# A sorted mixture of experts: inverting the order on chip, and one indirect DMA a block each way

## The reference

```python
x = x + tanh(g_xattn[0]) * attention(layernorm(x), ctx_768, ...)   # 16 heads, 1601 keys a batch
x = x + tanh(g_ffn[0]) * ffn(layernorm(x), ...)

def ffn(x, ...):                        # 8 experts, inner size 512
    shared = expert(x, Wg_s, Wu_s, Wd_s)   # silu(x @ Wg.T) * (x @ Wu.T) @ Wd.T
    probs = sigmoid(x @ Wr.T + rb)
    scores, idx = top_k(probs, 2)
    cw = (one_hot(idx, 8) * scores[..., None]).sum(-2)
    out = shared
    for e in range(8):
        out = out + cw[..., e:e + 1] * expert(x, Wg[e], Wu[e], Wd[e])
    return out
```

## Time and profile before

| | |
|---|---|
| time, median of 3 runs | 1178.47 us (1176.94 to 1181.26) |
| profiled execution, device time | 1180.16 us |
| its span | 1178.4 us |
| its mean granted TensorE clock | 0.957 |
| PE busy | 1095.5 us, 93% |
| DVE busy | 657.3 us, 56% |
| ACT busy | 570.7 us, 48% |
| POOL busy | 136.2 us, 12% |

### The profile page before, as it was taken

The page is one execution under the profiler, slowest core; times in us unless marked ns, Lnnn a source line. Parts: engine busy times, 40 slices in busy tenths (PEclk is TensorE's granted clock), DMA queues, the critical chain, the costliest instruction groups (busy, mean ns, idle before and its releaser), DMA issues. The chain is left out here.

```text
span 1178.4 us, 15206 instructions
## 1 busy us (share of the span) xinstructions
PE 1095.5 (93%) x5534; PEld 534.8 (45%) x5534; DVE 657.3 (56%) x895; ACT 570.7 (48%) x1056; POOL 136.2 (12%) x156
## 2 busy tenths in 40 slices
PE   4879999999999999999999999978869999999983
PEld 2433335434434433534433433435536666666652
DVE  4598776886676787677797685103412222222245
ACT  2107776776676776567777577623111111111110
POOL 4500000020000002000000003200550000000055
PEclk9859999999999999999999999859989999999998
DMA  9753505531505532505333501005820111111125
GB/s 314 114 93 38 60 1 61 102 46 16 61 1 60 96 39 30 61 1 60 38 41 45 59 3 59 5 5 174 321 94 18 45 45 45 46 45 45 36 72 151
DMA packets 51129, 78.08 MB, mean 66 GB/s; under 512 B 10993, under 2 KB 36210, under 8 KB 51058
## 3 DMA queue, kind: packets, MB, share of 16 engines
q1 hardware_dynamic: 45184, 66.87, 29.9%
q0 software_dynamic: 3072, 8.39, 2.2%
q10 hardware_dynamic: 2802, 1.85, 0.6%
HBM read 32.34 MB, written 16.52 MB: 41 GB/s over the span
## 5 line engine op out<-in xcount | busy, mean ns | idle before, releaser
L521 ACT ACTIVATE probs<-ring_ps 128x512 f32<-128x512 f32 (+1 forms) x832 | 443.4, 597 | 184.4 <-PE ring_ps L651 179.9
L755 DVE TENSOR_REDUCE mpart<-s_ps 128x2 f32<-128x1024 f32 x384 | 457.9, 1219 | 100.4 <-PE s_ps L638 98.9
L651 PE MATMUL ring_ps<-qst,kst 64*128 64x512 f32 (+1 forms) x832 | 233.8, 471 | 3.7 <-ACT probs L521 3.1
L666 PE MATMUL pv_ps<-probs,vp 128*32 128x512 f32 (+2 forms) x1664 | 226.2, 617 | 0.7 <-ACT probs L521 0.7
L638 PE MATMUL s_ps<-kst,qst 63*128 63x512 f32 (+1 forms) x1024 | 194.2, 419 | 11.8 <-DVE mpart L755 11.6
L651 PEld LDWEIGHTS ring_ps<-qst,kst 64*128 64x128 f32 (+1 forms) x832 | 102.4, 183 | 216.5 <-ACT probs L521 98.8
L962 ACT ACTIVATE s_sb<-gu_ps 128x512 f32<-128x512 f32 x55 | 32.8, 597 | 277.6 <-PE gu_ps L1039 277.6
L1039 PE MATMUL gu_ps<-wgu,xbT 128*128 x312 | 140.3, 593 | 0.0
L638 PEld LDWEIGHTS s_ps<-kst,qst 63*128 63x128 f32 x1024 | 95.6, 194 | 90.6 <-DVE mpart L755 68.9
L1168 DVE TENSOR_TENSOR h_sb<-s_sb,gu_ps 128x512 f32<-128x512 f32 x55 | 37.8, 687 | 174.8 <-ACT s_sb L962 174.8
L430 POOL COPY rspread<-rden 128x512 f32<-128x512 f32 x16 | 9.8, 612 | 674.6 <-DVE rden L798 674.6
(11 more groups left out here) (128 smaller groups left out, 712.2 us busy)
## 6 DMA issues: line engine op xcount, KB each, us to landing
kst<-parts SPq DMA_DIRECT2D x64, 200.5 KB, 4.4
kst<-parts SPq DMA_DIRECT2D x64, 100.2 KB, 4.2
sorted_x<-zeros SPq DMA_DIRECT2D x1, 4992.0 KB, 19.7
xb<-sorted_x SPq DMA_DIRECT2D x39, 128.0 KB, 2.2
sorted_y<-ysb SPq DMA_DIRECT2D x39, 128.0 KB, 1.7
qst<-parts SPq DMA_DIRECT2D x64, 64.0 KB, 4.2
wgu<-in_WgT SPq DMA_DIRECT2D x16, 256.0 KB, 7.9
wgu<-in_WuT SPq DMA_DIRECT2D x16, 256.0 KB, 8.1
```

Of the source, the lines that this page charges most:

```text
L521: nc.scalar.activation(probs[0:w, m % NPB, h, :], ring_ps[0:w, bank(("st", idx)), :], ACT.Exp, scale=SCALE).then_inc(exp_done, 1)
L651: nc.tensor.matmul(ring_ps[0:w, bank(("st", idx)), :], kst[u % NKB][rows, h // 2, mt * P:mt * P + w], qst[u % NKB][rows, h // 2, :], start ...
L666: last = nc.tensor.matmul(pv_ps[32 * h:32 * h + c1 - c0, :], values[:, c0:c1], probs[0:w, m % NPB, h, :], start=(mt == 0), stop=(mt == MT ...
L755: nc.vector.tensor_reduce(mpart[:, heads, t, q], s_ps[:, n % NSP], AX.X, ALU.max).then_inc(s_free, 1)
```

## The change

The scattered copy of the rows is gone. The normalised rows are stored to DRAM in token order (`rows`), 12 tiles by one DMA of SP during the last unit of attention and the last four by ACT in step 0. The sorted order is turned round on chip: for each of the 32 (choice, tile) pairs DVE makes two one-hot tiles from the slots, 128x128 (the row in a block) and 128x40 (the block, times the pair's number), and PE adds up the 32 products (`inverse`, before gate_up(4)), which gives for every row of every block the number of the pair it holds, or zero for padding. `make_lists` makes `token` (which row to fetch) and `target` (where its result goes) from it. Eight one-hot pairs are made in step 2 (ring of `NHOT` = 8), 24 in step 4.

GpSimd then fetches each block with one gather from `rows` by `token` and stores its result with one scatter to `picked` by `target`, where results lie in the order (choice, token); padding rows go to places of their own behind. SP does no block DMAs any more. When all scatters have landed it reads `picked` back in eight plain DMAs of 512 KB into the space of four experts' weights. Seven shared tiles stand before the blocks and nine after (`EARLY` = 7); combines are spread over seven steps from the fourth step after the last block's first; output stores come in the order in which tiles are finished. The clearing of the DRAM buffer is gone.

```diff
-NYG = 4
-EARLY = 10
-GATHER_ORDER = list(range(EARLY, TT)) + list(range(EARLY))
+EARLY = 7
+ASIDE = EARLY + 2
+COMBINE_ORDER = list(range(ASIDE, TT)) + list(range(ASIDE))
+SLOTS = TOP * B * N
+NCOL = NBLK + NBLK % 2
+NHOT = 8
 LAST = slice(TT - NT, TT)
-AT_LOGITS, AT_RANKS = 1, 2
+AT_LOGITS, AT_RANKS, AT_INVERSE = 1, 2, 4
 STK = 3 * HD
 NKB = 3
     return i - NBLK if i >= EARLY + NBLK else None
+
+
+def combines(i):
+
+    step, steps = i - (EARLY + NBLK + 3), TT - EARLY - 2
+    return range(TT * step // steps, TT * (step + 1) // steps) if 0 <= step < steps else range(0)
+
+
+def stores():
+
+    done = []
+    for i in range(TT + NBLK + 2):
+        done += [(COMBINE_ORDER[n], "combined", n + 1) for n in combines(i) if COMBINE_ORDER[n] < ASIDE]
+        t = tile_of(i - 2) if i >= 2 else None
+        if t is not None and t >= ASIDE:
+            done.append((t, "y_out", i - 1))
+    return done
 
...
                                  mneg[NT * h:NT * (h + 1), :].bitcast(F32)).then_inc(row_loaded[u % NKB], 16)
 
             sp.wait_ge(pool_ready, 3)
-                         zeros[:, None, :].to_broadcast([P, NBLK, D])).then_inc(zeroed, 16)
...
                     load_rows(u + 1)
+                else:
+                    sp.wait_ge(xn2_ready, NT * (B - 1))
+                    sp.dma_start(rows_dram[0:LAST.start * P, :].rearrange("(t p) d -> p t d", p=P),
+                                 xn2[:, 0:LAST.start, :]).then_inc(rows_stored, 16)
                 if hg == 2 and b + 2 < B:
                     load_ctx(b + 2)
...
+        hot_blk = sb("hot_blk", [P, NHOT, NCOL], F32R)
+        hot_row = sb("hot_row", [P, NHOT, P], F32R)
+        picked = wgu[:, 0:B].rearrange("p b k n -> p b (k n)").rearrange("p b (c t d) -> p b c t d", c=2, d=D)
...
 
-            def load_block(r):
-                if r >= NXB:
-                    sp.wait_ge(t_full, r - NXB + 1)
-                sp.dma_start(xb[:, r % NXB, :], xg_dram[r * P:(r + 1) * P, :]).then_inc(xb_loaded[r % NXB], 16)
-
-            sp.wait_ge(scattered, 16 * 2 * TT)
-            for r in range(NXB - 1):
-                load_block(r)
-            for r in range(NBLK):
-                if r + NXB - 1 < NBLK:
-                    load_block(r + NXB - 1)
-                sp.wait_ge(y_out, EARLY + r + 1)
-                sp.dma_start(yg_dram[r * P:(r + 1) * P, :], ysb[:, r % NXB, :]).then_inc(y_stored[r % NXB], 16)
-            for n, t in enumerate(GATHER_ORDER[TT - EARLY:]):
-                sp.wait_ge(combined, TT - EARLY + n + 1)
-                sp.dma_start(O["out"][t // NT, (t % NT) * P:(t % NT + 1) * P, :], x1[:, t, :]).then_inc(out_done, 16)
-            for n, t in enumerate(range(EARLY, TT)):
-                sp.wait_ge(y_out, EARLY + NBLK + n + 1)
+            for i in range(NXB):
+                sp.wait_ge(y_stored[i], 16 * ((NBLK - 1 - i) // NXB + 1))
+            for b in sorted(range(B), key=lambda b: COMBINE_ORDER.index(b * NT + NT - 1)):
+                for c in range(2):
+                    at = c * B * N + b * N
+                    sp.dma_start(picked[:, b, c], picked_dram[at:at + N, :].rearrange("(t p) d -> p t d", p=P)
+                                 ).then_inc(picked_loaded[b], 16)
+            for t, engine_sem, count in stores():
+                sp.wait_ge(combined if engine_sem == "combined" else y_out, count)
                 sp.dma_start(O["out"][t // NT, (t % NT) * P:(t % NT + 1) * P, :], x1[:, t, :]).then_inc(out_done, 16)
             sp.wait_ge(out_done, 16 * TT)
 
         @block.gpsimd
         def _(pool):
             nc.gpsimd.memset(ones[:], 1.0).then_inc(consts, 1)
-            nc.gpsimd.iota(count_i[:], pattern=[[1, NBLK]], base=0, channel_multiplier=0).then_inc(consts, 1)
+            nc.gpsimd.iota(count_i[:], pattern=[[1, NCOL]], base=0, channel_multiplier=0).then_inc(consts, 1)
 
             nc.gpsimd.iota(tri_i[:], pattern=[[1, E], [-1, E]], base=0, channel_multiplier=0).then_inc(consts, 1)
             pool.wait_ge(consts, 3)
 
             nc.gpsimd.affine_select(out=lower[:], in_=ones[:], compare_op=ALU.is_gt, fill=0.0, base=0,
                                     pattern=[[1, P]], channel_multiplier=-1).then_inc(consts, 1)
+            nc.gpsimd.iota(col_i[:], pattern=[[1, P]], base=0, channel_multiplier=0).then_inc(consts, 1)
+            nc.gpsimd.iota(id_i[:], pattern=[[B * N, 2], [P, TT]], base=1, channel_multiplier=1).then_inc(consts, 1)
+            nc.gpsimd.iota(trash_i[:], pattern=[[P, NBLK]], base=SLOTS + 1, channel_multiplier=1).then_inc(consts, 1)
             rstd_on_pool(nc, pool, LAST, mv, veps, rstd, power, ln, 1, sq, 0)
-            pool.wait_ge(xn2_ready, NT)
-            pool.wait_ge(slots_ready, 1)
-            for t in range(TT):
-                for c in range(2):
-                    pool.indirect_dma_start(xg_dram[:], bass.IndirectOffsetOnAxis(ap=slot_i[:, c, t:t + 1], axis=0),
-                                            xn2[:, t, :], None).then_inc(scattered, 16)
-            for i in range(NXB):
-                pool.wait_ge(y_stored[i], 16 * ((NBLK - 1 - i) // NXB + 1))
-            for n, t in enumerate(GATHER_ORDER):
-                if n >= NYG:
-                    pool.wait_ge(combined, n - NYG + 1)
-                for c in range(2):
-                    pool.indirect_dma_start(yg[:, n % NYG, c, :], None, yg_dram[:],
-                                            bass.IndirectOffsetOnAxis(ap=slot_i[:, c, t:t + 1], axis=0)
-                                            ).then_inc(gathered[n % NYG], 16)
+
+            def gather(r):
+                if r >= NXB:
+                    pool.wait_ge(t_full, r - NXB + 1)
+                pool.indirect_dma_start(xb[:, r % NXB, :], None, rows_dram[:],
+                                        bass.IndirectOffsetOnAxis(ap=token[:, r:r + 1], axis=0)
+                                        ).then_inc(xb_loaded[r % NXB], 16)
+
+            pool.wait_ge(rows_stored, 16)
+            pool.wait_ge(token_ready, 1)
+            for r in range(NXB - 1):
+                gather(r)
+            pool.wait_ge(target_ready, 1)
+            for r in range(NBLK):
+                if r + NXB - 1 < NBLK:
+                    gather(r + NXB - 1)
+                pool.wait_ge(y_out, EARLY + r + 1)
+                pool.indirect_dma_start(picked_dram[:], bass.IndirectOffsetOnAxis(ap=target[:, r:r + 1], axis=0),
+                                        ysb[:, r % NXB, :], None).then_inc(y_stored[r % NXB], 16)
 
         @block.scalar
         def _(act):
...
                     silu(i)
+                if i == 0:
+                    act.wait_ge(xn2_ready, NT)
+                    act.dma_start(rows_dram[LAST.start * P:LAST.stop * P, :].rearrange("(t p) d -> p t d", p=P),
+                                  xn2[:, LAST, :]).then_inc(rows_stored, 16)
                 if i >= 1:
                     take_ht(i - 1)
...
                 nc.tensor.matmul(t_ps[:, at + n:at + 2 * n], ones[:], flat, start=True, stop=True
                                  ).then_inc(rank_full, 1)
+
+            def inverse():
+                at = 3 * TT * E
+                for n in range(2 * TT):
+                    pe.wait_ge(hot_ready, n + 1)
...
 
             for i in range(JOBS + 2):
+                if i == AT_INVERSE:
+                    inverse()
...
-            dve.wait_ge(consts, 4)
+            dve.wait_ge(consts, 7)
+            nc.vector.tensor_copy(col[:], col_i[:])
...
                     own(nc.vector.tensor_reduce(slot_f[:, c], pick[:], AX.X, ALU.add))
-                nc.vector.tensor_copy(slot_i[:], slot_f[:]).then_inc(slots_ready, 1)
-
-                own(nc.vector.tensor_tensor(past[:, :, 0:E - 1], rows_f[:, :, None].to_broadcast([P, NBLK, E - 1]),
+                own(nc.vector.tensor_copy(slot_i[:], slot_f[:]))
+                own(nc.vector.tensor_scalar(lane_i[:], slot_i[:], P - 1, None, ALU.bitwise_and))
+                own(nc.vector.tensor_copy(lane[:], lane_i[:]))
+                own(nc.vector.tensor_tensor(first_row[:], slot_f[:], lane[:], ALU.subtract))
+
+            def make_hot(jobs):
+
+                for n in jobs:
+                    c, t = divmod(n, TT)
+                    if n >= NHOT:
+                        dve.wait_ge(hot_used, n - NHOT + 1)
+                    nc.vector.tensor_scalar(hot_row[:, n % NHOT, :], col[:], lane[:, c, t:t + 1], None, ALU.is_equal)
+                    nc.vector.tensor_scalar(hot_blk[:, n % NHOT, :], rows_f[:], first_row[:, c, t:t + 1],
+                                            ids[:, c, t:t + 1], ALU.is_equal, ALU.mult).then_inc(hot_ready, 1)
+
+            def make_lists():
+
+                dve.wait_ge(hot_used, 2 * TT)
+                own(nc.vector.tensor_copy(held[:], t_ps[:, 3 * TT * E:3 * TT * E + NBLK]))
+                own(nc.vector.tensor_scalar(second[:], held[:], float(B * N), float(-B * N), ALU.is_gt, ALU.mult))
```

(44 more changed lines are left out.)

35 lines of the change are left out of this document (23 added, 12 removed).

## The result

On the chip of the prediction's runs the changed kernel takes 1210.46 us (median of 4 runs, 1208.67 to 1215.59) and the kernel before 1177.70 (4 runs, 1173.60 to 1181.26): ratio 1.0286, 95% interval 1.024 to 1.0333. It is slower by 2.9%, as forecast (1218, range 1186 to 1236). On another chip, on which the kernel before takes longer, the ratio is 1.0164 (see the experiments). The profiled execution took 1211.1 us, with a span of 1209.4.

A forecast was written before the change was run, and what follows sets the result against it. PE bounds the kernel, so its standstills in the expert stage count: +63.4 blocks, -2.7 old stalls, -2.2 head, -16.6 tail, -2.4 stores = +39.5; 1180.16 becomes 1219.7, minus 1.7 gives 1218 us, range 1186 to 1236.

The forecast's parts named there:

- Blocks: Expert blocks: take_y to landed block exceeds the allowed 3.17 us by 1.81, period 7.63, 35 x 1.81 = +63.4; old stalls replaced, -2.7.
- 4.98 us "word for word": Blocks: release-to-data time of two indirect DMAs behind one wait, read from the old read back, taken as the new chain.
- half case: Blocks: GpSimd wakes quickly, chain 4.10 us, +32.6 instead of +63.4, time 1187; chance 0.17 (1184 to 1208).
- main case: Blocks: chain from take_y to data near 5 us, time 1208 to 1232; chance 0.62.
- the quick wake: Blocks: GpSimd starts at the release, chain 4.10 us, +32.6, time 1187; range 1184 to 1208, chance 0.17.
- Hidden wait: Blocks, rival: descriptor preparation or generation overlaps, chain within 3.17 us, period 5.82, sum -23.9, time 1155; chance 0.13.
- Clock: Blocks, rival: idle PE drops to 1.2 GHz in each block, +1.7 a block, 60 in all, 1278; chance 0.05.
- Head: List stage before the blocks: inverse costs +11.1, lost stall gives -13.3, together -2.2, between -4 and +2.
- The stall of 13.3: List stage: PE time lost around 32 indirect scatters before the first block, expected to go entirely.
- The upper bound of the prediction (+2): Head: worst end of -4 to +2, with pairs at 0.41 us and PE perhaps returning at lower clock, 1.4.
- Tail and stores: After the blocks: 16.6 of 21.2 us lost come back; one final store left instead of six, -2.4.
- Attention: Before the experts: dropping the 5 MB clear (19.7 us to land) and storing rows during attention each change 0.

## Why the prediction was right

**Blocks: the mechanism right, its price too high.** Forecast 35 waits and a period of 7.63; measured 35 and, typically, 7.03. The term that was mis-sized is the choice of 4.98 us "word for word" for the chain from take_y to data. Gather after scatter (1.29) and rows after the gather (2.78) came as read from the earlier trace rows; the start of the scatter came 0.28 after its release and not 0.88. The two places that gave 0.88 and 0.90 were waits of GpSimd for several semaphores, and two waits in place of one give the dearer start back in the changed kernel. So the chain is 4.36, 1.19 over what is free, and 35 of them would be +42 where 63.4 was forecast; the quick start was the prediction's half case (4.10). The other 8 us are in late blocks: of the 35 periods over 5.82 (from transpose to transpose) eight exceed 7.5, and the last two are 8.33 and 8.79. Seven late landings, of up to 3.6 us, make some 5 of the 8, two starts at 0.76 and 0.77 make 1, and a stretch at lower clock after PE had stood 2.27 us 0.9:

```profile
1125.28 0.99 POOL L984 DMA_INDIRECT picked<-ysb,target  x1 [6.10 <-DVE ysb L1266]
1126.58 0.97 POOL L971 DMA_INDIRECT xb<-rows,token  x1 [0.30 <-issue]
...
1130.19 0.44 PE L1058 MATMUL t_ps<-ident,xb 128*128 128x128 f32 x2 [2.27 <-DMA xb<-rows,token]
1130.47 2.81 PE L1100 MATMUL y_ps<-wd,hT 128*128 x8
```

The late landings belong to certain blocks and not to a time. In all eight traces of kernels with the change, where the landing is recorded, the gathers of blocks 4, 23, 33 and 35 to 38 take 3.27 to 3.89 us, and the others 2.64 to 3.06, save one of 3.24. They are the blocks that are mostly or only padding: with its own inputs (seed 0) the reference gives these seven 117, 94, 97 and four times 128 padding rows, and no other block more than 26 (that the timed executions had these inputs is inferred from the match). Every padding row fetches row 0 of `rows` (`token` is 0 there), while in the scatters padding rows go to places of their own, and those of blocks 35 to 38 land in 2.40 to 2.61. That the shared row makes the gather late is argued from this: no run gave the padding rows different rows to fetch. With the gather ahead of the scatter the late landings cost nothing.

**What was luck.** That 1210 lies in the main case (1208 to 1232) owes something to misses that cancel. With 4.36 in place of 4.98, and all other terms as forecast, the sum gives 1196, which lies in the case of the quick wake; the late blocks (8) and the head (6.4) brought it back.

**Hidden wait: refuted.** It needed a chain of less than 3.85 us, and the chain is 4.36. The Trainium skill's fit (DMA: Bandwidth & Descriptors, Anatomy of one DMA) gives 2.3 us for 128 KB as an estimate, and the scatter's median landing, 2.4 us after its start in the trace, agrees. What decides here stands beside it in the trace: 0.28 to start, 1.30 for the scatter that is issued first, and 2.78 from the gather's start to PE going on.

**Clock: only at the edges.** PE stands 1.1 us in 7, and the granted clock of 876 to 1120 is 1.00. Idle times of about the same length went either way: after 2.27 us at 1130 it fell to 0.50, after 2.54 at 826 and 2.74 at 1205 the next product still ran at 1.00; in the second execution of the changed kernel that was traced it fell after 2.16 at 1201, in the one with two waits after 2.18 at 989.

**Head: wrong sign, +4.2 for -2.2.** The stall of 13.3 went. The inverse was dearer in three terms: the down product before it ran at half clock and began 0.6 later, which cost 2.3; 24 pairs took 9.8 us at 0.41 and not 7.9 at 0.33, since the 40 wide instruction, a third as wide as the other, starts 0.21 before the next one all the same; and gate_up(4), behind 11 us of waiting for pairs, took 2.1 more. Together 6.3, of 6.4 that were missed. The upper bound of the prediction (+2) had pairs at 0.41 but the clock for one product only.

**Tail and stores: as forecast**, -16.7 and -2.5. **Attention** gained 1.2 where 0 was forecast; the experts begin at 806.3 to 810.3 in four traces with the 5 MB clear and at 805.2 to 811.5 in eight without, so no gain from leaving out the clear is shown.

The misses are -13.5 for the blocks, +6.4 for the head, -1.2 for attention and -0.1 each for tail and stores: -8.5 of 39.5.

## What to carry to other kernels

On a queue that runs in order, ask of each transfer what it stands behind: a load issued behind a store inherits the store's wait, its start and its issue, and one block more of distance, by order or by a buffer, can make all of that free. When work moves to an engine with dearer issue, redo that sum with the slack that the old trace shows (3.17 us here), and take the price of a wake from a wait with as many semaphores as the new one has. Work for two engines in lockstep (one makes operands, the other consumes) costs the slower one's whole time if the other stands still for it (11.24 us here), and little in pieces behind jobs that are there anyway (1.2 us for a third of it).

## What the hardware showed

- GpSimd starts an indirect DMA 0.28 us after the release when one semaphore was to be waited for (37 of 39 scatters of the changed kernel), and 0.76 to 0.81 when two were, though one had long been there (37 of 39 of the kernel with two waits).
- An indirect gather of 128 rows of 1 KB lands 2.6 to 2.9 us after its start (the first of a kernel 3.0 to 3.1, one of the others 3.24), and 3.3 to 3.9 when 94 or more of the rows are the same one.
- A 128x40 tensor_scalar of DVE with two per-partition scalars starts 0.21 us before the next one, no sooner than a 128x128 with one scalar (0.20).
- The kernel before took 1178, 1195, 1196 and 1178 us on four chips (medians), the changed one 1210 and 1213 on the two where it was timed. In one execution of the former, of 1192 us, ScalarE and VectorE stood up to 15.6 us without a named cause while GpSimd issued its indirect DMAs.
